# Token tiles and output weights turned by transposing DMAs instead of TensorE, and the weight presets and additions of an attention-plus-MLP layer given new places

## The reference

```python
xn = layernorm(x)                                   # x: 2 x 1024 tokens x 1024
def bitnet_linear(x, w, scale):                     # signs of w, one scale per output channel
    s = max(mean(abs(w), axis=1), 1e-8)
    y = einsum('bsi,oi->bso', x, sign(w / s[:, None])) * (s * scale)
    return nan_to_num(y, nan=0.0, posinf=1e6, neginf=-1e6)
q, k, v = (bitnet_linear(xn, w, sc) for w, sc in ...)   # 1024, 256 and 256 channels
attn = softmax(q k^T / sqrt(32)) v                  # 32 heads of 32, 8 key/value heads
a = bitnet_linear(attn, o_weight, o_scale)
W = (int_w - zeros) * scales                        # groups of 128 rows, gate/up 1024x3584, down 3584x1024
m = (silu(xn @ Wgate) * (xn @ Wup)) @ Wdown
return x + a + m
```

## Time and profile before

| | |
|---|---|
| time before, median of 3 runs | 2332.88 us (2332.0 to 2333.92) |
| the profiled execution, its own time | 2336.82 us |
| its span, first to last instruction | 2335.0 us |
| PE busy | 2285.4 us (98%) |
| DVE, ACT, POOL busy | 1806.1, 1595.6, 1000.0 us |
| mean granted clock of PE | 0.996 |

### The profile page before, as it was taken

The page is one execution under the profiler, slowest core; times in us unless marked ns, Lnnn a source line. Parts: engine busy times, 40 slices in busy tenths (PEclk is TensorE's granted clock), DMA queues, the critical chain, the costliest instruction groups (busy, mean ns, idle before and its releaser), DMA issues.

```text
span 2335.0 us, 44858 instructions
## 1 busy us (share of the span) xinstructions
PE 2285.4 (98%) x18443; PEld 1101.4 (47%) x18443; DVE 1806.1 (77%) x2305; ACT 1595.6 (68%) x2059; POOL 1000.0 (43%) x567
## 2 busy tenths in 40 slices
PE   6899999999999999999999999999999999999998
PEld 4444455555545555534444444444445444444444
DVE  8879888888888888857577777777777777777777
ACT  5775788888888888872366666666666666666664
POOL 0450599999999999960022222210003222221000
PEclk9999999999999999999999999999999999999999
DMA  5892345444444444443211111121124111115111
GB/s 186 162 205 28 78 70 82 73 76 69 75 76 72 76 74 68 83 93 117 79 37 36 37 37 53 38 109 36 36 72 145 36 37 37 36 48 187 36 36 72
DMA packets 178305, 175.51 MB, mean 75 GB/s; under 512 B 87778, under 2 KB 127586, under 8 KB 178102
## 3 DMA queue, kind: packets, MB, share of 16 engines
q1 hardware_dynamic: 113590, 143.28, 19.7%
q0 software_dynamic: 64512, 29.37, 12.8%
HBM read 160.08 MB, written 65.45 MB: 97 GB/s over the span
## 4 chain that ended last, share of the span: by engine, by line
PE 90%; DVE 4%; ACT 3%; issue 1%; SPq 1%; DMA 1%; POOL 0%; DVEq 0%; ACTq 0%
PE ps L1704 33%; PE ps L1720 17%; PE ps L1476 9%; PE ps L1529 9%; PE ps L1543 9%; PE ps L1675 5%; PE ps L1558 5%; PE ps L1501 3%; ACT zone L825 1%; SPq L383 1%; DVE sm L1005 1%; DVE zone L1140 1%; DVE zone L1044 1%; PE ps L1736 0%; DMA zone<-zone 0%
## 5 line engine op out<-in xcount | busy, mean ns | idle before, releaser
L1704 PE MATMUL ps<-xT,zone 128*128 128x512 f16 x3584 | 774.2, 379 | 0.0
L1159 DVE TENSOR_REDUCE zone<-ps 128x1 f32<-128x512 f32 x1024 | 639.0, 682 | 126.9 <-PE ps L1476 118.7
L825 ACT ACTIVATE zone<-ps,sm 128x512 f32<-128x512 f32 x1024 | 628.1, 692 | 117.1 <-PE ps L1529 112.8
L654 POOL TENSOR_TENSOR zone<-zone 128x1024 f32<-128x1024 f32 x252 | 619.2, 2545 | 125.8 <-ACT zone L825 71.6
L1393 DVE TENSOR_SCALAR ps<-ps,zone_c 128x1024 f32<-128x1024 f32 x392 | 506.6, 1293 | 162.5 <-PE ps L1704 160.4
L948 ACT ACTIVATE ps<-ps,zone_c 128x1024 f32<-128x1024 f32 x392 | 426.6, 1088 | 248.2 <-PE ps L1704 248.2
L1704 PEld LDWEIGHTS ps<-xT,zone 128*128 128x128 f16 x3584 | 350.6, 98 | 422.5 <-DVE zone L1397 0.3
L1476 PE MATMUL ps<-zone 96*32 96x512 f16 (+1 forms) x3946 | 438.1, 381 | 8.3 <-issue 3.4
L1529 PE MATMUL ps<-zone 98*32 98x512 f16 x4096 | 438.6, 381 | 4.5 <-ACT zone L825 4.3
L1720 PE MATMUL ps<-zone 128*128 128x512 f16 x1792 | 387.1, 379 | 0.0
L1404 DVE TENSOR_SCALAR ps<-ps,zone_c 128x1024 f32<-128x1024 f32 x216 | 279.2, 1293 | 93.1 <-PE ps L1720 92.9
(11 more groups left out here) (140 smaller groups left out, 1403.7 us busy)
## 6 DMA issues: line engine op xcount, KB each, us to landing
zone<-dequantised SPq DMA_DIRECT2D x84, 512.0 KB, 3.6
dequantised<-zero_points SPq DMA_DIRECT2D x56, 256.0 KB, 3.9
zone<-zone SPq DMA_DIRECT2D x384, 32.0 KB, 2.3
zone<-_attn_hidden_states_dram SPq DMA_DIRECT2D x16, 512.0 KB, 7.2
zone<-inverse_sums SPq DMA_DIRECT2D x128, 64.0 KB, 2.1
attention<-zone SPq DMA_DIRECT2D x32, 256.0 KB, 2.0
xT<-attention SPq DMA_DIRECT2D x4, 2048.0 KB, 12.3
dequantised<-zero_points POOLq DMA_DIRECT2D x28, 256.0 KB, 11.1
```

What stands on the lines that cost most here:

```text
L654: nc.gpsimd.tensor_tensor(duo[n % 3], prob[:, prob_slot(e), :], prob[:, prob_slot(e + 2), :], add).then_inc(s["sum_ok"], 1)
L825: A(prob[:, prob_slot(e), m % 2 * 512:(m % 2 + 1) * 512], ps[:, 3 + m % 3, :], ACT.Exp, scale=gam[:, 0:1]).then_inc(s["exp_ok"], 1)
L1159: V.tensor_reduce(mxs[:, u % 2, half, i % 16:i % 16 + 1], ps[:, (2 * i + half) % 3, :], AX, amax).then_inc(s["max_ok"], 1)
L1704: last = MM(ps[:, 4 * s2 + 2 * m + c, :], ring[:, buf, m * H + g * P:m * H + (g + 1) * P], xT[:, hf, part, g, c * 512:(c + 1) * 512], star ...
```

## The change

- **Tokens.** The tiles 4 to 15 (chunks 1 to 3) are no longer turned on PE. SP issues two transposing DMAs for each tile, one for the high half when `h_ok` says that it is written, one for the low half (`l_ok`); 24 DMAs of 256 KB, from SBUF to SBUF. 192 transposes of PE and 24 copies of ACT go. `high(i)` and `low(i)` now wait until the DMA of tile i-2 has landed, `project(c, 0)` until the DMAs of the chunk have. DVE does `low` one output earlier. 
- **Where they stand on SP.** Tiles 4 to 7 behind `load_x(2)`, with the store of the zero points (and its wait) between tiles 6 and 7; then the loads of the tiles 12 to 15, then tiles 8 to 11. Tile 12 stands behind `store_kv(0)`, tile 13 behind `load_k(0)` and `load_q(0)`, tiles 14 and 15 behind `load_v(0)` and `load_k(1)`; `load_q(1)` and `load_q(2)` follow.
- **Output weights.** The eight tiles are turned by transposing DMAs too. The one of tile 0 is issued behind all of SP's steps of the attention, and `attend_output(0)` waits for it; tile 1 behind the loads of weights 2 to 5; tile i (from 2) ahead of the store of output 2i-3.
- **Presets and additions.** All 84 presets are issued by SP in the attention, one every sixth step. POOL issues no DMA before the end of the attention: additions 0 to 3 follow its last steps for unit 30, 4 to 23 those for unit 31, and three more follow each `split_hidden` of the MLP's first 28 tiles. `load_block` of the first half waits for its own pieces.
- `turn_values` and the first `row_scores` get waits of their own where the order used to follow from the turns.

The core of the diff (removed code that only mirrors this is left out):

```diff
-FIRST_WEIGHTS = 28
-ADD_BEHIND = {4 + (9 * m + 1) // 2: FIRST_WEIGHTS + m for m in range(TILES - FIRST_WEIGHTS)}
+WEIGHTS_AHEAD = 24
...
+            def turn_tile(i):
+
+                to = slice((i % 8) * P, (i % 8 + 1) * P)
+                if i == 8:
+                    sp.wait_ge(s["z_out"], 16)
+                sp.wait_ge(s["h_ok"], i + 1)
+                sp.dma_start_transpose(xT[:, i // 8, 0, :, to], hst[:, i % 2, :]).then_inc(s[f"xh_in{i % 2}"], 16)
+                sp.wait_ge(s["l_ok"], i + 1)
+                sp.dma_start_transpose(xT[:, i // 8, 1, :, to], lst[:, i % 2, :]).then_inc(s[f"xl_in{i % 2}"], 16)
...
-            sp.wait_ge(s["z_ok"], 1)
-            sp.dma_start(zscr.rearrange("t m c -> t (m c)"), zf16).then_inc(s["z_out"], 16)
-            load_x(3)
+            for j in range(4):
+                turn_tile(4 + j)
+                if j == 2:
+                    sp.wait_ge(s["z_ok"], 1)
+                    sp.dma_start(zscr.rearrange("t m c -> t (m c)"), zf16).then_inc(s["z_out"], 16)
+            for j in range(4):
+                load_tile(12 + j)
+            for j in range(4):
+                turn_tile(8 + j)
...
             store_kv(0)
+            turn_tile(12)
             sp.wait_ge(s["kv_out"], 32)
             load_k(0)
+            load_q(0)
+            turn_tile(13)
             load_v(0)
-            load_q(0)
+            load_k(1)
+            turn_tile(14)
+            turn_tile(15)
             load_q(1)
             load_q(2)
-            load_k(1)
...
+            def turn_wo(i):
+                sp.wait_ge(s["wosgn_ok"], i + 1)
+                sp.dma_start_transpose(woT[:, i, :].rearrange("p (t c) -> p t c", t=KT), wosg[:, i % 2, :]).then_inc(s[f"woT_in{i % 2}"], 16)
+
             def preset_weights(n):
...
-                if e % 9 == 0 and FIRST_WEIGHTS + e // 9 < TILES:
-                    preset_weights(FIRST_WEIGHTS + e // 9)
+                if e % 6 == 0 and e // 6 < TILES:
+                    preset_weights(e // 6)
...
+                if hf == 0:
+                    for n in ((3 * j, 3 * j + 1) if j < IT else [3 * t + 2 for t in range(4 * q, 4 * q + 4)]):
+                        sp.wait_ge(s[f"weights{n % 4}"], 16 * (n // 4 + 1))
                 sp.dma_start(dst, src).then_inc(s[f"wr_in{buf}"], 16)
...
+            sp.wait_ge(s["snat_pe"], 1)
+            turn_wo(0)
             sp.wait_ge(s["pv_pe"], round_of(UNITS - 1, 5) + 1)
...
             load_wo(5)
+            turn_wo(1)
+            sp.wait_ge(s["pv_pe"], round_of(UNITS - 1, 7) + 1)
             for n in range(OUTPUTS):
+                if n % 2 == 1 and 2 <= (n + 3) // 2 < FQ:
+                    turn_wo((n + 3) // 2)
...
             for u in range(UNITS - 2, UNITS):
                 divide(u)
                 tail_of(u)
+                for n in range(4) if u < UNITS - 1 else range(4, WEIGHTS_AHEAD):
+                    add_weights(n)
...
                     split_hidden(hf, t)
+                    if hf == 0:
+                        for n in range(WEIGHTS_AHEAD + 3 * t, min(WEIGHTS_AHEAD + 3 * t + 3, TILES)):
+                            add_weights(n)
...
             def high(i):
                 act.wait_ge(s["xc_ok"], i + 1)
+                if i >= 6:
+                    act.wait_ge(s[f"xh_in{i % 2}"], 16 * ((i - 4) // 2))
+                elif i >= 2:
+                    act.wait_ge(s["xh_pe"], i - 1)
...
                         elif p == 6:
-                            evac_high(i)
                             high(i + 2)
                         elif p == 7:
-                            evac_low(i)
-                            evac_high(i + 1)
                             high(i + 3)
...
-                        elif (7 if c == 0 else 6) <= p < 10:
-                            low(i + p - 6)
+                        elif (6 if c == 0 else 5) <= p < 9:
+                            low(i + p - 5)
...
+                elif p == 0:
+                    for j in range(2):
+                        pe.wait_ge(s[f"xh_in{j}"], 32 * c)
+                        pe.wait_ge(s[f"xl_in{j}"], 32 * c)
...
-                    if c + 1 < NC:
-                        if p == 6:
-                            pe.wait_ge(s["v_out"], 2 * c + 2)
-                            turn_high(i)
-                        elif 7 <= p < 10:
-                            turn_low(i + p - 7)
-                            turn_high(i + p - 6)
-                        elif p == 10:
-                            turn_low(i + 3)
...
-                    pe.wait_ge(s["woT_out"], ot + 1)
+                    pe.wait_ge(s[f"woT_in{ot % 2}"], 16 * (ot // 2 + 1))
...
-                if n % 2 == 0 and n // 2 + 1 < FQ:
-                    turn_output_weights(n // 2 + 1)
```

More of the change, by code:

```diff
@@ L454, in preset_weights @@
                 if n >= 4:
-                    sp.wait_ge(s[f"weights{n % 4}"], 16 * (n // 4))
+                    sp.wait_ge(s[f"preset{n % 4}"], 16 * (n // 4))
                 sp.dma_start(wscr[t, m, :, :], zscr[t, m, :].partition_broadcast(P)).then_inc(s[f"preset{n % 4}"], 16)
@@ L552, in _ @@
                 elif n == 12:
-                    for j in range(4):
-                        sp.wait_ge(s[f"weights{j}"], 16 * (TILES // 4))
                     sp.wait_ge(s["wosgn_ok"], 5)
@@ L616, in add_weights @@
                 t, m = n // 3, n % 3
[L617 to L620, removed]
+                pool.wait_ge(s[f"preset{n % 4}"], 16 * (n // 4 + 1))
+                if n >= 4:
+                    pool.wait_ge(s[f"weights{n % 4}"], 16 * (n // 4))
                 if m < 2:
@@ L626, in add_weights @@
                 nc.gpsimd.dma_start(dst, src, accum_op=add, max_dma_last_dim=4096).then_inc(s[f"weights{n % 4}"], 16)
[L628 to L640, removed]
             pool.wait_ge(s["kv_out"], 32)
@@ L898, in output_signs @@
                 if i >= 2:
[L899 removed]
+                    act.wait_ge(s[f"woT_in{i % 2}"], 16 * (i // 2))
                 A(wosg[:, i % 2, :], woraw[i], ACT.Sign).then_inc(s["wosgn_ok"], 1)
@@ L1051, in low @@
                 dve.wait_ge(s["h_ok"], i + 1)
-                if i >= 2:
+                if i >= 6:
+                    dve.wait_ge(s[f"xl_in{i % 2}"], 16 * ((i - 4) // 2))
+                elif i >= 2:
                     dve.wait_ge(s["xl_pe"], i - 1)
@@ L1472, in row_scores @@
                     pe.wait_ge(s["max_ok"], c - 2)
+                else:
+                    pe.wait_ge(s["y_ok"], max(n for n in range(36) if output_bank(n) == c) + 1)
                 wide = P if i < LEAD else 32
@@ L1489, in project @@
                     wait_weights(pe, p)
-                if p == 0:
-                    pe.wait_ge(s["xh_out"], 4 * (c + 1))
-                    wait_low_parts(pe, 4 * (c + 1))
+                if p == 0 and c == 0:
+                    pe.wait_ge(s["xh_out"], 4)
+                    wait_low_parts(pe, 4)
+                elif p == 0:
+                    for j in range(2):
+                        pe.wait_ge(s[f"xh_in{j}"], 32 * c)
+                        pe.wait_ge(s[f"xl_in{j}"], 32 * c)
                 if n == 46:
@@ L1512, in turn_values @@
                     pe.wait_ge(s["r_ok"], 12 * c + fv + 1)
-                    if fv == 0:
-                        pe.wait_ge(s["xh_out"], 4 * (c + 1))
+                    if c:
+                        pe.wait_ge(s["v_out"], 2 * (c - 1) + fv + 1)
+                    elif fv == 0:
+                        pe.wait_ge(s["xh_out"], 4)
                     else:
-                        wait_low_parts(pe, 4 * (c + 1))
+                        wait_low_parts(pe, 4)
                     for t in range(4):
@@ L1581, in spread_maxima @@
                 last.then_inc(s["pmr_pe"], 1)
-            def turn_output_weights(i):
-                pe.wait_ge(s["wosgn_ok"], i + 1)
-                if i >= 2:
-                    pe.wait_ge(s["woT_out"], i - 1)
-                for t in range(KT):
-                    last = TR(bank16(2 + i % 2)[:, t * P:(t + 1) * P], wosg[:, i % 2, t * P:(t + 1) * P], id16[:])
-                last.then_inc(s["woT_pe"], 1)
             turn_weights(0)
@@ L1657, in _ @@
                     spread_maxima()
-                if u == UNITS - 1 and k == 9:
-                    turn_output_weights(0)
             values(UNITS - 1, 7)
```

38 lines of the change are left out of this document (11 added, 27 removed).

## The result

The changed kernel takes 2338.47 us (median of 17 runs) beside 2333.95 us for the kernel before on the same chip: a ratio of 1.0018, 95% interval 1.0011 to 1.0025. It is slower by some 4 us, where 2325.4 and a gain were forecast. The profiled execution took 2338.28 us, 2336.5 of them span.

What follows compares the result with a forecast made beforehand. PE was taken to bound the kernel, with 90% of the chain that ended last. Terms: -5.2 - 0.9 - 3.0 - 1.0 + 2.0 = -8.1, taken as -7.5 from 2332.9: 2325.4 us; range 2318 to 2346, the forecast's own 2319 to 2329.

Steps and rivals of the forecast that it cites:

- end of chunk 0: Projections: tile 7 lands earlier (-2.6), half clock behind the start of chunk 1 costs +1.7; -0.9 us.
- chunk 1: Projections: eight turns (3.6) and 1.6 us of waits go from PE; -5.2 us.
- chunk 2: Projections: turns and waits of 4.9 us go, outputs held behind `high(15)` cost +1.9; -3.0 us.
- chunk 3 and attention: Everything shifts as a whole from chunk 3; attention gains from departing additions and one turn, -1.0 us, bounds 0 and -3.
- output projection: Seven turns go (-3.2), but `turn_wo(0)` makes PE wait before output 0, with half clock; +2.0 us in all.
- MLP: Additions moved there cost 0; the MLP should keep its length to within a microsecond, about 1183 us.
- Cost of a transposing DMA: On SP, per 256 KB: 0.6 us of issue (bounds 0.5 to 2.0), 3.5 us to landing (2.3 to 6.9).
- rival of the slow queue: SP's queue: issue of 2 us makes turns late, chunk 2 deciding; 2337.6 us; chance 0.28 together with late landing.
- The first wait: Output projection: PE waits 3.5 us before output 0 for the transposing DMA, bounds 2.3 and 7.
- 6.5 us from issue to need: Output projection: time the other weight tiles have from issue to need, except tile 3 with 5 us.
- Additions at their new place: End of attention and MLP: POOL has time and pieces are done before they are needed; cost 0.
- slow queue or late landing: SP's queue: 2 us of issue gives 2337.6; landing after 6.9 us costs about +6 against before; chance 0.28.

Runs made afterwards that it cites:

- A with W: Presets and additions moved and output weights turned by DMA, tokens still turned on PE, against the kernel before: 2335.61 us, ratio 1.0010.
- A with T: Presets and additions moved and token tiles turned by DMA, output weights still turned on PE, against the kernel before: 2328.45 us, ratio 0.9980.
- the three parts: Presets and additions moved alone, against the kernel before: 2327.54 us; with token tiles by DMA added, 2328.45; with output weights by DMA added instead, 2335.61.

## Why the prediction was wrong

The steps of the sum, forecast and as the two traces have them (us; the projections from turn of values to turn of values, the last one to the end of the attention):

| step | forecast | traces |
|---|---|---|
| end of chunk 0 | -0.9 | +1.0 |
| chunk 1 | -5.2 | -5.6 |
| chunk 2 | -3.0 | +5.4 |
| chunk 3 and attention | -1.0 | -7.1 |
| output projection | +2.0 | +7.4 |
| MLP | 0 | +1.4 |

They add up to +2.5; the trace of the kernel before entered chunk 0 a microsecond later, which leaves the 1.5 between the spans.

**Chunk 1: right.** Forecast -5.2; between the turns of values in chunks 1 and 2 it is -5.6 (42.3 us, before 48.0).

**Cost of a transposing DMA: landing right, issue mis-sized.** Taken: 3.5 us to land and 0.6 to issue. Measured: 3.3 to 3.4 undisturbed, and 1.27 to 1.33 us of issue (medians of the two lines), so that this term of the sum was half of what it should be. It is just short of the 1.4 us from which the rival of the slow queue was to decide, but that rival isn't the cause either: with the same issue time and another order the tokens bring 10 us. Advanced Engine Details and Errata of the Trainium skill, X-Bar Transpose (TRN2), says that these DMAs are as fast as others; for the landing the trace agrees (3.4 us beside 4.0 for a preset of the same size), for the issue it does not (1.27 beside 0.59 us). By VectorE: DVE Perf Modes of the Trainium skill, The three transpose paths, taken block by block, a landing would be an estimated 10.5 us; the trace is far below that.

**End of chunk 0: +1.0 in place of -0.9.** From the turn of values in chunk 0 to that in chunk 1 it is 54.6 us (before: 53.6). The waits of PE (2.73 + 3.28 + 3.44 = 9.5 us) have the size that I expected, and the half clock came, but the cause is another, so the match is luck: not tile 7 behind the zero points but DVE's `place_weights(11)` came last. It released the last output of chunk 0 at 82.67. What was left out is that `load_x(2)` holds the issue too (3.99 us for the first DMA of tile 4), and that DVE's `low(6)` waits behind ACT's `high(6)`.

**Chunk 2: +5.4 in place of -3.0. This step failed.** The place was right: `high(15)` waiting for tile 13 behind `load_q(0)`. Its price was not. I let PE run on over its six banks and charged 1.9 us, for outputs held back on ACT. In the trace that wait is 1.41 us. Not priced were DVE, held for 8 us behind ACT (4.63 us on PE, for the row maxima), the queries themselves, late for the first early scores (1.70), and the half clock that follows: from 179.14 to 186.18 PE takes 7.0 us for what takes 4.5 at full clock. Waits of 7.7 and half clock of 2.5, less the 4.9 of turns and waits that went, are the +5.4. I had followed the engine that waits to what is queued behind it, but not the second engine that waits for the first. With the order mended chunk 2 gives what the turns and waits were said to be worth: 4.4 us by the turns of values (53.02 less 48.66), forecast 4.9.

**Attention: -7.1 in the traces, in place of -1.0.** I put most of PE's idle time down to DVE and ACT. The windows hid a part of what there was to gain: PE's idle time fell only by 4.4 us (13.6 to 9.1). The row that mattered was in hand: landings of `load_q` up to 6.9 us, used only as a bound for something else. In the kernel before, PE's early scores had these waits between 262 and 1030 (line, what it waits for: us in total, times, longest), 4.9 us; in the changed kernel they are gone:

```profile
PE ps L1476 <- issue: 3.4, 3, 1.5
PE ps L1476 <- DMA zone<-zone: 1.5, 1, 1.5
```

How much of the 7.1 holds for the median is less sure. From the turn of values in chunk 3 to the end of the attention the kernel before took 832.6 us in its one trace, 2.9 us above its median in all, where the two other kernels with 56 additions in the attention took 826.9 and 828.5, and the changed kernel 825.5.

**Output projection: +7.4 in place of +2.0. The second step that failed.** The first wait was 2.14 us and its half clock came, within the forecast. What failed is the other tiles. Their landing takes 5.2 us in the median and up to 10.2, not 3.5, and "6.5 us from issue to need" was short for two of them: tile 6 had 6.8 (issued at 1073.39, needed at 1080.2), but tiles 1 and 3 only 4.0, tile 1 because of the loads ahead of it. So four tiles are waited for (1.30 + 0.86 + 1.17 + 3.09 = 6.4 us). In A with W the additions held back leave tile 1 as the only one of these that is waited for (1.35 us): that wait is order, the others are late landings.

**Additions at their new place: 0 was wrong.** In the MLP the zero stands: its +1.4 us in this pair of traces (1184.1, before 1182.7) is no sign of them, since A with T, with the same additions, has 1182.7 as well. But the additions make the transposing DMAs of the output weights late: held back until those have landed, they give 7.0 us back. POOL's time and the pieces' due times were checked, the other users of the DMA engines were not.

Of the rivals, "slow queue or late landing" comes nearest, with its 2337.6: late landings in the output projection, and a queue that is late in one place, because of its order and not of its issue times. That its number is met within a microsecond is luck: it was worked out from 2 us of issue or 6.9 us of landing, and neither was measured (1.3; medians of 3.4 for the tokens, 5.2 for the weights).

**Open:** why additions make transposing DMAs late. Shown is that they do, and that with all 84 presets on SP in the attention `load_q` still lands after 1.9 us; whether packets, the issue of POOL or the path into SBUF is the bottleneck was not tried. Nor is it shown that accumulation matters: beside the plain 2 MB of `load_x(2)`, with nothing of POOL in flight, the first DMA of tile 4 took 3.99 us to issue and 7.5 to land, so that any heavy traffic may do it. The sum of the three parts (-5.6 +0.9 +8.1 = +3.4) agrees with the +4.5 of the whole within the intervals.

## What to carry to other kernels

When work moves from an engine to DMAs, write down the order of the issuing queue with times. Give a long run of small loads that are ready a place where the queue is idle, so that no transfer that others wait for stands behind it: here one exchange of lines was worth 11.5 us. Follow a late buffer through two engines, since an engine that waits in order holds back what a third one needs. And count accumulating DMAs as neighbours of every short transfer whose landing is on the path: in the attention they cost some 4 us, 2 to 3 of them seen as late queries, in the output projection 7 through the weights.

## What the runs showed of the hardware

- A transposing DMA of 256 KB from SBUF to SBUF took SP 1.23 us at least to issue and landed after 3.0 to 3.1 us at least.
- Beside POOL's additions and presets in the projections its issue took up to 7.96 us and its landing up to 16.9; beside the additions of the output projection the issue stayed at 1.3 us in the median (2.7 at most), and the median landing went from 3.2 to 5.2 or 5.7 us.
- Plain traffic does it too: behind `load_x(2)` (2 MB) one such DMA took 3.99 us to issue and 7.5 to land.
- Small loads are delayed too: `load_q` (32 KB) landed after 1.9 us in the median with no addition in the attention, 2.3 with 56 of them.
